# Window attention: the band mask moved to TensorE, and subtraction, copies, layer norm and mask rows moved to GpSimd

## The chip, the cores and the metric

The kernel runs on one core of one Trainium2 chip. The metric is device time in microseconds (us). One execution was profiled, and all durations of the trace come from it. TensorE (PE) has two clock levels, 1.2 and 2.4 GHz; a granted clock of 0.50 in a stretch is the lower one, 1.00 the upper.

## What is computed

Two stages follow each other, each on 8 batches of 1024 rows of width 256. The first is window attention with 16 heads of width 16, then a residual and a layer norm:

```python
scores = jnp.einsum('bhqd,bhkd->bhqk', q, k) / math.sqrt(dh)
scores = jnp.exp(scores - jnp.max(scores, axis=-1, keepdims=True))   # maximum over all 1024 keys
mask = (d <= half - 1) & (d >= -half)                                # d = j - i, half = 32
scores = jnp.where(mask, scores, 0.0)
weights = jax.nn.softmax(scores, axis=-1)                            # softmax of the exponentials
out = jnp.einsum('bhqk,bhkd->bhqd', weights, v)
x = _layernorm(x + out.transpose(0, 2, 1, 3).reshape(B, S, H * dh) @ Wo)
```

Outside the band the inner exponential is set to 0, so its own exponential is 1. The output is therefore (sum of all v + the sum over the band of (e^e^s - 1) v) divided by its mass. The second stage routes each row through three small trees and attends over the results. The change does not touch it.

## The kernel before

The work of the first stage is cut into units: unit u = 2b + g is half g (8 heads) of batch b, and one unit is 64 steps, eight steps of 128 queries for each head. Each engine has its instructions written out in one order, step by step, with semaphores between the engines. Batches 2 to 6 run in a loop, the others are written out.

In every step PE makes one `p_diff` (L529) and one `p_half` (L533), both 128x512. ScalarE (ACT) takes the positive part of `p_diff` into `above` (L615). VectorE (DVE) adds the two and takes the row maximum (L724). PE runs one `p_diff` ahead.

The rest hangs on the steps by lags. "Lag n" of head h of the unit before is step 8h + n of this unit, or step 8h + n - 64 of the one after.

- Lag 9: PE computes the window scores `p_win` (L545), 16 products of 64 columns. Each block of 64 queries sees 128 keys. The rows with the negated maxima (`m_parts`) have to be in `q_stack` before head 0's.
- Lags 10 and 11: first exponential, in two halves of 512 (L641). Lags 12 and 13: second exponential, two halves (L638).
- Lags 13 and 14: DVE computes `w_win = (p_win - 1) * window` in two halves (L758), where `window` is the 0/1 band.
- Lags 15 and 16: PE multiplies `w_win` with the values (L558, `p_pv`). Lag 18: DVE adds the value sum (L777). Lag 19, odd heads: DVE takes the reciprocal (L750), GpSimd (POOL) scales the pair into `att` (L421).

Beside this a list of jobs, `JOBS`, has one job every four steps: "m" transposes the maxima, "q", "k", "d" make the next unit's projections and split them into bf16 parts, "V" and "S" the values and their sum, "T", "O", "X" transpose `att`, project it, and transpose the next x. Job j begins at step 4j + 1 on PE. ACT and DVE follow one step later, POOL at step 4j + 4, and ACT's middle part (L627, `s_mid`) comes at step 4j + 5. For "q", "k" and "d" the POOL waits at step 4j + 4 for that middle part and then makes the low part (L398). DVE copies one part (L739), and the SP queue then loads `q_stack`, `k_stack` and `d_stack` head by head (L328).

At step 4 POOL makes two of the three bf16 parts of the negated maxima (L388, L390). At the start of the next unit SP's queue waits for them and issues three row transfers into `q_stack` (L271).

The layer norm of batch b - 2 has its statistics in unit (b - 1, 1). POOL computes `rstd` (L428, L430) at the start of unit (b, 0), and DVE normalises eight tiles of 128x256 at steps 1 to 8 (L710). SP then stores x1 and loads the next x.

## Time and profile before

| | us |
|---|---|
| median of 3 runs | 2668.9 (2658.05 to 2669.55) |
| the profiled execution's own time | 2644.6 |
| its span | 2642.8 |
| first to last row maximum (16 units) | 49.4 to 1440.8 |
| last normalisation issued | 1521.0 |
| second stage's first instruction | 1528.5 |
| PE, DVE, ACT, POOL busy | 2100.6, 1811.0, 1392.7, 659.4 |

A unit takes (1440.8 - 49.4) / 16 = 87.0 us. The time that an engine is busy is a union of its instructions' durations, so two that overlap in its pipeline count once. The median of the runs is 24.3 us above the profiled execution.

### The profile page before, as it was taken

What the parts mean: (1) busy time and instruction counts of PE and PEld (TensorE: products, weight loads), DVE (VectorE), ACT (ScalarE), POOL (GpSimd) and SP (SyncE); (2) the same over time, 40 slices, a digit from 0 to 9 for tenths busy, and PEclk for the clock granted to TensorE, in tenths of its full rate; (3) what the DMA queues carried; (4) which work ended last, traced back from release to release, by engine and by line L of the source; (5) the groups of instructions that cost most, each with busy time, mean ns of one, the idle gap of its engine ahead of it and who ended that gap; (6) DMA issues with size and microseconds to landing.
All of it is one profiled execution on the core that took longest, in us unless ns stands there. A gap on an engine that the chain in (4) does not pass through costs nothing. (4 is left out here: it accounts for less than half of the span.)

```text
span 2642.8 us, 46194 instructions
## 1 busy us (share of the span) xinstructions
PE 2100.6 (79%) x13533; PEld 1602.7 (61%) x13533; DVE 1811.0 (69%) x4451; ACT 1392.7 (53%) x2671; POOL 659.4 (25%) x920
## 2 busy tenths in 40 slices
PE   4779888788788898887888668356468848999998
PEld 2345556455555555564555657346467748999997
DVE  3667788778787787787968335536558745777775
ACT  3557667757666676676756212124246533444442
POOL 3110111101111111111100035555521135556511
PEclk8878888989888888898978555667679879999999
DMA  4624643565346435543470081699977742333311
GB/s 72 94 47 67 111 56 62 88 94 70 64 73 111 54 59 94 83 63 70 68 111 18 17 259 70 212 380 341 287 253 248 231 151 84 88 98 100 97 53 39
DMA packets 230094, 306.36 MB, mean 116 GB/s; under 512 B 44445, under 2 KB 145866, under 8 KB 229450
## 3 DMA queue, kind: packets, MB, share of 16 engines
q1 hardware_dynamic: 186746, 199.14, 37.5%
q0 software_dynamic: 22784, 67.13, 7.9%
q10 hardware_dynamic: 20304, 36.97, 3.7%
q8 instruction: 120, 1.97, 0.3%
q14 instruction: 140, 1.15, 0.1%
HBM read 129.33 MB, written 92.27 MB: 84 GB/s over the span
## 5 line engine op out<-in xcount | busy, mean ns | idle before, releaser
L724 DVE CUSTOM_DVE_ANT_0 above<-p_half,above 128x512 f32<-128x512 f32 x1024 | 691.3, 684 | 305.6 <-issue 248.1
L615 ACT ACTIVATE above<-p_diff 128x512 f32<-128x512 f32 x1024 | 599.4, 600 | 269.4 <-PE p_diff L529 267.6
L529 PE MATMUL p_diff<-d_stack,q_stack 96*128 96x512 bf16 x1024 | 433.3, 426 | 127.0 <-ACT above L615 96.0
L533 PE MATMUL p_half<-k_stack,q_stack 96*128 96x512 bf16 x1024 | 431.8, 422 | 31.0 <-DVE row_max L724 27.2
L558 PEld LDWEIGHTS p_pv<-v_win,w_win 128*128 128x128 f32 x2048 | 312.0, 225 | 78.0 <-DVE w_win L758 52.6
L558 PE MATMUL p_pv<-v_win,w_win 128*128 128x34 f32 x2048 | 307.6, 302 | 14.5 <-DVE w_win L758 13.0
L529 PEld LDWEIGHTS p_diff<-d_stack,q_stack 96*128 96x128 bf16 x1024 | 127.0, 125 | 285.3 <-ACT above L615 206.4
L1170 POOL DMA_INDIRECT raw<-sorted_y,place x192 | 206.2, 1074 | 238.5 <-DMA sorted_y<-y_tile 182.9
L641 ACT ACTIVATE p_win<-p_win 128x512 f32<-128x512 f32 x256 | 150.3, 589 | 181.5 <-PE p_win L545 179.9
L421 POOL TENSOR_TENSOR att<-total,inv 128x128 f32<-128x128 f32 x128 | 48.9, 404 | 759.2 <-DVE inv L750 759.2
L1492 ACT ACTIVATE pt_hi<-p_one 128x512 fp32r<-128x512 f32 x128 | 69.6, 595 | 259.6 <-PE p_one L1352 243.9
L758 DVE SCALAR_TENSOR_TENSOR w_win<-p_win,window 128x512 f32<-128x512 f32 x256 | 175.1, 684 | 17.9 <-ACT p_win L638 17.7
L533 PEld LDWEIGHTS p_half<-k_stack,q_stack 96*128 96x128 bf16 x1024 | 107.2, 105 | 114.7 <-DVE row_max L724 96.8
L1271 PE MATMUL p_one<-ident,x_tile 128*128 128x128 f32 x564 | 97.1, 301 | 82.2 <-DMA x_tile<-sorted_x 82.1
L545 PE MATMUL p_win<-q_stack,k_stack 99*128 99x64 bf16 x2048 | 101.2, 211 | 71.1 <-DMA q_stack<-m_parts 62.6
L638 ACT ACTIVATE p_win<-p_win 128x512 f32<-128x512 f32 x256 | 153.5, 603 | 0.0
L1663 DVE TENSOR_TENSOR tile_t_lo<-p_one,tile_t_hi 128x512 fp32r<-128x512 f32 x141 | 96.6, 685 | 80.2 <-issue 41.3
L1206 PE MATMUL p_out<-val_hi,pt_hi 128*128 128x256 f32 x512 | 150.7, 294 | 0.7 <-DVE sum L1748 0.7
L545 PEld LDWEIGHTS p_win<-q_stack,k_stack 99*128 99x128 bf16 x2048 | 90.4, 111 | 97.3 <-issue 53.2
L1206 PE MATMUL p_out<-val_hi,pt_lo 128*128 128x256 f32 x512 | 145.2, 284 | 0.0
L1206 PE MATMUL p_out<-val_lo,pt_hi 128*128 128x256 f32 x512 | 145.2, 284 | 0.0
L1416 ACT ACTIVATE tile_t_hi<-p_one 128x512 fp32r<-128x512 f32 x141 | 83.5, 592 | 112.6 <-PE p_one L1271 49.9
(217 smaller groups left out, 4857.1 us busy)
## 6 DMA issues: line engine op xcount, KB each, us to landing
x_tile<-sorted_x SPq DMA_DIRECT2D x141, 256.0 KB
sorted_y<-y_tile ACTq DMA_DIRECT2D x141, 256.0 KB
q_stack<-q_parts SPq DMA_DIRECT2D x256, 96.0 KB, 3.1
k_stack<-k_parts SPq DMA_DIRECT2D x256, 96.0 KB, 3.7
x_in<-in_L_attn_x SPq DMA_DIRECT2D x16, 1024.0 KB, 5.5
x_rows<-x POOLq DMA_DIRECT2D x16, 1024.0 KB
sorted_x<-zeros SPq DMA_DIRECT2D x51, 256.0 KB
d_stack<-d_parts SPq DMA_DIRECT2D x256, 48.0 KB, 3.7
```

What stands on the lines that cost most here:

```text
L529: nc.tensor.matmul(p_diff[s % 2][:], qs, d_stack[0:SPLIT_ROWS, h, :], start=True, stop=True).then_inc(s_diff, 1)
L533: nc.tensor.matmul(p_half[s % 2][:], qs, k_stack[g][0:SPLIT_ROWS, h, HALO + S // 2:HALO + S], start=True, stop=True).then_inc(s_half, 1)
L545: ins = nc.tensor.matmul(p_win[:, cols], k_stack[o][0:ROWS, h, WIN * i:WIN * i + P], q_stack[o][0:ROWS, h, cols], start=True, stop=True)
L558: ins = nc.tensor.matmul(p_pv[:, 2 * DV * t:2 * DV * t + 2 * DV].rearrange("p (n d) -> p n d", n=2), w_win[:, h % 2, P * t:P * t + P], v_w ...
L615: nc.scalar.activation(above[:, s % 4], p_diff[s % 2][:], ACT.Relu).then_inc(s_above, 1)
L638: nc.scalar.activation(p_win[:, cols], p_win[:, cols], ACT.Exp).then_inc(s_e2, 1)
L641: nc.scalar.activation(p_win[:, cols], p_win[:, cols], ACT.Exp, scale=DH ** -0.5).then_inc(s_e1, 1)
L724: nc.vector.tensor_tensor_reduce(out=above[:, s % 4], in0=p_half[s % 2][:], in1=above[:, s % 4], scale=1.0, scalar=-3.0e38, op0=ALU.add, o ...
L758: nc.vector.scalar_tensor_tensor(w_win[:, h % 2, cols].rearrange("p (i j) -> p i j", j=WIN), p_win[:, cols].rearrange("p (i j) -> p i j", ...
L1170: pool.indirect_dma_start(raw[b % 2][:, n, t, :], None, ys[n][:, :], bass.IndirectOffsetOnAxis(ap=where, axis=0), bounds_check=OUT_ROWS - ...
L1206: ins = nc.tensor.matmul(out_, l, r, start=first and n == 0, stop=last and n == 2)
L1271: ins = nc.tensor.transpose(p_one[j % 2][:, TILE * c + P * t:TILE * c + P * t + P], xr[:, j % X_TILES, t, P * c:P * c + P], ident[:])
```

## The change

It does five things. (1) PE adds the band mask to the window scores: for each bank of `p_win` one more product, bf16 identity times `outside` (0 inside the band, -30000 outside), repeated over 8 blocks, 512 columns. After the scale of 1/4 the first exponential gives 0 there and the second gives 1. (2) The exponentials are two instructions of 1024 columns each at lags 10 and 11, and the second writes `w_win`. POOL subtracts 1 in place, 128x1024, at lag 12, and DVE's L758 is gone. (3) The three rows of maxima go out from POOL's queue right after their parts are made. SP no longer waits for them. (4) The copies L739 move from DVE to POOL, behind L398. (5) The eight normalisations move from DVE (steps 1 to 8, one instruction each) to POOL (steps 4 to 11, a subtraction, a wait for it, and a multiplication each, both with a broadcast operand).

```diff
-EXP_LAGS = 10, 11, 12, 13
-WEIGHT_LAGS = 13, 14
+EXP_LAGS = 10, 11
+WEIGHT_LAG = 12
 @@ sync
-                    wait_alone(sp, s_mparts, u)
-                    for part in range(3):
-                        row = SPLIT_ROWS + part
-                        sp.dma_start(q_stack[1 - g][row:row + 1, :, :],
-                                     m_parts[:, part, :]).then_inc(s_mrow, 16)
 @@ gpsimd, job "m", behind m_parts
+                            pool.wait_ge(s_mparts, u)
+                            wait(pool, s_win, GH * (u - 2))
+                            alone(pool)
+                            for part in range(3):
+                                row = SPLIT_ROWS + part
+                                pool.dma_start(q_stack[1 - g][row:row + 1, :, :],
+                                               m_parts[:, part, :]).then_inc(s_mrow, 16)
 @@ gpsimd, jobs "q", "k", "d", and behind the jobs
+                            copy, of = (0, 1) if kind == "q" else (3, 2)
+                            nc.gpsimd.tensor_copy(parts[:, copy, cols], parts[:, of, cols]).then_inc(s_twice, 1)
+                    for w, o, h in late(b, g, s, WEIGHT_LAG):
+                        weights(GH * w + h, h)
                     for w, o, h in late(b, g, s, PAIR_LAG):
                         if h % 2:
                             pair(b, g, w, h // 2)
+                    if g == 0 and has(b, 2, B + 1) and 4 <= s < 4 + QT:
+                        normalise(b - 2, s - 4)
+            def normalise(b, q):
+                if q == 0:
+                    wait_alone(pool, s_rstd, b + 1)
+                row_mean = mean_var[:, q, 0:1].to_broadcast([P, C])
+                nc.gpsimd.tensor_tensor(y[:, q], y[:, q], row_mean, ALU.subtract).then_inc(s_centre, 1)
+                wait_alone(pool, s_centre, QT * b + q + 1)
+                nc.gpsimd.tensor_tensor(y[:, q], y[:, q], rstd[:, q:q + 1].to_broadcast([P, C]),
+                                        ALU.mult).then_inc(s_norm, 1)
+            def weights(k, h):
+                wait_alone(pool, s_e2, k + 1)
+                nc.gpsimd.tensor_scalar(w_win[:, h % 2], w_win[:, h % 2], -1.0, None, ALU.add).then_inc(s_ww, 1)
             batches(pool, unit)
             spread(B - 1)
+            for q in range(QT):
+                normalise(B - 1, q)
 @@ tensor, window_scores and weighted_values
-                wait(pe, s_ww, 2 * k)
+                wait(pe, s_e2, k)
+                    if i % 8 == 0:
+                        bank = p_win[:, 64 * i:64 * i + 512].rearrange("p (i j) -> p i j", j=WIN)
+                        nc.tensor.matmul(bank, ident_b[:], outside[:].unsqueeze(1).to_broadcast([P, 8, WIN]),
+                                         start=True, stop=False, skip_group_check=True)
-                pe.wait_ge(s_ww, 2 * k + part + 1)
+                if part == 0:
+                    pe.wait_ge(s_ww, k + 1)
 @@ scalar, exponential
-                    nc.scalar.activation(p_win[:, cols], p_win[:, cols], ACT.Exp).then_inc(s_e2, 1)
+                    wait(act, s_pv, k - 1)
+                    nc.scalar.activation(w_win[:, h % 2], p_win[:], ACT.Exp).then_inc(s_e2, 1)
 @@ vector
-                        normalise(b - 2, s - 1)
-                            nc.vector.tensor_copy(parts[:, copy, cols], parts[:, of, cols]).then_inc(s_twice, 1)
-                nc.vector.scalar_tensor_tensor(
-                    w_win[:, h % 2, cols].rearrange("p (i j) -> p i j", j=WIN),
-                    p_win[:, cols].rearrange("p (i j) -> p i j", j=WIN), 1.0,
-                    window[:].unsqueeze(1).to_broadcast([P, NBLK // 2, WIN]),
-                    ALU.subtract, ALU.mult).then_inc(s_ww, 1)
```

Three places show how the rows move. The first is POOL's order from step 4 to the projection jobs of unit (7, 0), which is written out; the loop has the same. Before:

```order
L388 CAST m_parts<-m_rest 64x128
L390 TENSOR_TENSOR m_parts<-m_rest,m_parts 64x128
L421 TENSOR_TENSOR att<-total,inv 128x8x16 x2
L398 TENSOR_TENSOR q_parts<-rest,q_parts 128x512
L421 TENSOR_TENSOR att<-total,inv 128x8x16 x2
```

The same place after the change, where `x_in` is the tile that is normalised (eight pairs of L447 and L449 in all, of which the first and the last stand here):

```order
L386 CAST m_parts<-m_rest 64x128
L388 TENSOR_TENSOR m_parts<-m_rest,m_parts 64x128
L395 DMA q_stack<-m_parts 1x64x128 x3
L454 TENSOR_SCALAR w_win<-w_win 128x1024
L447 TENSOR_TENSOR x_in<-x_in,mean_var 128x256
L449 TENSOR_TENSOR x_in<-x_in,rstd 128x256
...
L432 TENSOR_TENSOR att<-total,inv 128x8x16 x2
L447 TENSOR_TENSOR x_in<-x_in,mean_var 128x256
L449 TENSOR_TENSOR x_in<-x_in,rstd 128x256
L454 TENSOR_SCALAR w_win<-w_win 128x1024 x2
```

Between the maxima's parts and the first pair of `att` shown (the last head pair of an earlier unit) there are now three DMA issues, one subtraction of 1 and seven normalisations. It is the pair that job T waits for.

The second place is POOL in the stretch of the projection jobs of the same unit, after the change (before, it had the L398 rows and the pairs alone):

```order
L403 TENSOR_TENSOR q_parts<-rest,q_parts 128x512
L406 COPY q_parts<-q_parts 128x512
L454 TENSOR_SCALAR w_win<-w_win 128x1024
L403 TENSOR_TENSOR k_parts<-rest,k_parts 128x512
L406 COPY k_parts<-k_parts 128x512
L403 TENSOR_TENSOR k_parts<-rest,k_parts 128x512
L406 COPY k_parts<-k_parts 128x512
L454 TENSOR_SCALAR w_win<-w_win 128x1024
```

At steps 28 and 36 of a unit the subtraction L454 stands behind a low part and a copy, both of which wait for ACT's step 29 or 37.

The third place is PE at the window scores of one head, before and after (L529 and L556 are the same line, as are L533 and L560):

```order
L533 MATMUL p_half<-k_stack,q_stack 128x512
L545 MATMUL p_win<-q_stack,k_stack 128x64 x16
L529 MATMUL p_diff<-d_stack,q_stack 128x512
L533 MATMUL p_half<-k_stack,q_stack 128x512
L529 MATMUL p_diff<-d_stack,q_stack 128x512
```

```order
L560 MATMUL p_half<-k_stack,q_stack 128x512
L574 MATMUL p_win<-outside,ident_b 128x512
L576 MATMUL p_win<-q_stack,k_stack 128x64 x8
L574 MATMUL p_win<-outside,ident_b 128x512
L576 MATMUL p_win<-q_stack,k_stack 128x64 x8
```

Each head has two more products of 512 columns, one ahead of each eight blocks, and nothing else moves on PE.

## Rows read from the trace of the kernel before

**Rows 1.** The maximum's instruction L724 by source line.

```profile
L724 DVE CUSTOM_DVE_ANT_0 above<-p_half,above x1024: 625/691/694, 49.4 to 1440.8; 128x512 f32<-128x512 f32 x171
```

**Rows 2.** Stretches of 4 us in batch 2: busy by engine, then granted clock.

```profile
core 0: us, PE busy (x) PEld busy (x) DVE busy (x) ACT busy (x) POOL busy (x), PEclk, DMA share, GB/s
...
434.00:438.00 4.00, 2.63 (x11) 0.81 (x9) 3.88 (x11) 3.95 (x9) 0.12 (x1) 0.99 0.00 0
442.00:446.00 4.00, 4.00 (x18) 3.54 (x16) 1.75 (x6) 1.71 (x3) 1.15 (x1) 0.50 0.02 4
```

**Rows 3.** L724 alone, two records for each step, in stretches of 4 us.

```profile
431.00:435.00 4.00, 2.33 (x8) 1.00 0.00 0
443.00:447.00 4.00, 1.14 (x4) 0.50 0.00 0
```

**Rows 4.** Groups, 0 to 1350 us: busy, mean ns; idle before, its releasers.

```profile
L529 PE MATMUL p_diff<-d_stack,q_stack 96*128 96x512 bf16 x953 | 400.7, 423 | 123.4 <-ACT above L615 92.7 <-DMA d_stack<-d_parts 13.4 <-issue 12.2
L758 DVE SCALAR_TENSOR_TENSOR w_win<-p_win,window 128x512 f32<-128x512 f32 x220 | 150.3, 683 | 0.0
L641 ACT ACTIVATE p_win<-p_win 128x512 f32<-128x512 f32 x220 | 129.8, 590 | 137.5 <-PE p_win L545 136.2
L739 DVE COPY k_parts<-k_parts 128x512 bf16<-128x512 bf16 x32 | 25.4, 794 | 0.8 <-ACT k_parts L627 0.7
```

**Rows 5.** Timeline around the maxima's rows in unit (2, 1): start, us, engine.

```profile
480.03 0.42 POOL L390 TENSOR_TENSOR m_parts<-m_rest,m_parts 64x128 bf16<-64x128 f32 x1
481.53 1.08 PE L558 MATMUL p_pv<-v_win,w_win 128*128 128x34 f32 x8
488.70 1.82 SPq L271 DMA_DIRECT2D q_stack<-m_parts x3
492.36 1.03 PE L545 MATMUL p_win<-q_stack,k_stack 99*128 99x64 bf16 x16 [7.86 <-DMA q_stack<-m_parts]
```

**Rows 6.** The rows' transfers by tile: who waited, and time to landing.

```profile
  PE p_win L545: 62.6, 8
...
DMA to landing us min/median/max: 2.2/2.5/3.4
```

**Rows 7.** Timeline of unit (2, 0), steps 3 to 13.

```profile
396.82 0.28 DVE L669 SCALAR_TENSOR_TENSOR m_rest<-p_job,m_parts 64x128 f32<-64x128 f32 x1
408.46 0.20 PEld L465 LDWEIGHTS p_job<-ident,att 128*128 128x128 f32 x2 [0.64 <-POOL att L421]
```

**Rows 8.** POOL groups of the whole span.

```profile
L421 POOL TENSOR_TENSOR att<-total,inv 128x128 f32<-128x128 f32 x128 | 48.9, 404 | 759.2 <-DVE inv L750 759.2
L398 POOL TENSOR_TENSOR k_parts<-rest,k_parts 128x512 bf16<-128x512 f32 x32 | 37.3, 1166 | 122.9 <-ACT k_parts L627 122.9
L1151 POOL DMA_DIRECT2D x_rows<-x x16 | 15.1, 942 | 70.8 <-DMA sorted_x<-x_rows,slot 70.8
L408 POOL COPY v_sum<-v_sum 128x136 f32<-128x136 f32 x8 | 2.4, 296 | 0.0
L1127 POOL MEMSET w<- 128x1024 f32 x1 | 0.9, 945 | 0.0
```

**Rows 9.** Timeline of steps 29 to 31 of unit (2, 0).

```profile
426.88 0.63 ACT L627 ACTIVATE q_parts<-rest 128x512 bf16<-128x512 f32 x1
427.92 1.09 ACT L615 ACTIVATE above<-p_diff 128x512 f32<-128x512 f32 x2
429.56 1.08 PE L558 MATMUL p_pv<-v_win,w_win 128*128 128x34 f32 x8 [0.38 <-DVE w_win L758]
```

**Rows 10.** Timeline, 512-column products behind each other at granted clock 1.00.

```profile
404.72 0.38 PE L529 MATMUL p_diff<-d_stack,q_stack 96*128 96x512 bf16 x1
404.94 0.38 PE L533 MATMUL p_half<-k_stack,q_stack 96*128 96x512 bf16 x1
```

**Rows 11.** ACT's 1024-column group of the second stage.

```profile
L1387 ACT ACTIVATE w<-w 128x1024 fp32r<-128x1024 f32 x18 | 19.0, 1056 | 7.1 <-DMA b<-in_L_ffn_q_b 6.8
```

**Rows 12.** Timeline of the first stage's end.

```profile
1521.03 2.67 DVE L710 TENSOR_SCALAR x_in<-x_in,mean_var,rstd 128x256 f32<-128x256 f32 x8 [2.19 <-POOL rstd L430]
```

More of the change, by code:

```diff
@@ L113, in window_attention @@
         ones = sb("ones", [P, 1])
-        window = sb("window", [P, WIN])
+        ident_b = sb("ident_b", [P, P], BF16)
+        outside = sb("outside", [P, WIN], BF16)
         neg_half = sb("neg_half", [P, QT])
@@ L199, in window_attention @@
         s_rstd = sem("rstd_ready")
+        s_centre = sem("x1_less_mean")
         s_norm = sem("x1_ready")
@@ L264, in unit @@
                 if g == 1 and has(b, -1, 0):
[L265 to L272 removed]
+                    wait_alone(sp, s_const, 18)
                 if g == 0 and has(b, -1, 0):
@@ L347, in _ @@
             const(nc.gpsimd.memset(ident[:], 0.0))
-            const(nc.gpsimd.memset(window[:], 1.0))
+            const(nc.gpsimd.memset(outside[:], 0.0))
             pool.wait_ge(s_const, 2)
@@ L726, in unit @@
                             op0=ALU.add, op1=ALU.max, accum_out=row_max[g][:, s:s + 1]).then_inc(s_max, 1)
-                    if g == 0 and has(b, 2, B + 1) and 1 <= s <= QT:
-                        normalise(b - 2, s - 1)
                     for j, kind, i in jobs(b, g, s, 2):
@@ L731, in unit @@
                             job(b, g, j, kind, i)
-                    for j, kind, i in jobs(b, g, s, 4):
-                        if kind in PROJ:
-                            dve.wait_ge(s_mid, before(PROJ, b, g, j) + 1)
-                            parts = {"q": q_parts, "k": k_parts, "d": d_parts}[kind]
-                            copy, of = (0, 1) if kind == "q" else (3, 2)
-                            cols = slice(512 * i, 512 * i + 512)
-                            nc.vector.tensor_copy(parts[:, copy, cols], parts[:, of, cols]).then_inc(s_twice, 1)
-                    for n in (0, 1):
-                        for w, o, hh in late(b, g, s, WEIGHT_LAGS[n]):
-                            weights(GH * w + hh, hh, n)
                     for w, o, hh in late(b, g, s, TOTAL_LAG):
@@ L783, in _ @@
             batches(dve, unit)
-            for q in range(QT):
-                normalise(B - 1, q)
 NETS = 3
```

36 lines of the change are left out of this document (15 added, 21 removed).

## The prediction

> **What bounds the kernel now.** I read the instruction L724 first, because every step has one. The 16 units run from its first record to its last, 87.0 us for a unit and 1.36 us for a step [rows 1]. All that the change touches lies there, but for the first stage's last layer norm. Then I cut a batch into stretches of 4 us. The reader is to see that the bound changes within a unit, and twice over. At 434 to 438 us DVE is busy 3.88 and ACT 3.95 of 4.00 while PE has 2.63, and at 442 to 446 PE has 4.00 at granted clock 0.50 while the other two have less than half [rows 2]. Of the 45 stretches between 390 and 570 us, 20 have DVE at 3.84 or more, of which this one is an example, and PE is busy 3.38 on average in them. The maxima show what the low clock costs: 4 steps in 4 us at the high one, 2 at the low one [rows 3].
>
> Third, the groups. PE idles 92.7 us for ACT before `p_diff`, ACT idles 136.2 us for PE before the first exponential, and DVE never idles before L758 [rows 4]. So PE and ACT take turns in waiting for each other, and DVE adds its delay in its full stretches. Fourth, the waits on the maxima's rows. In unit (2, 1) the parts are ready at 480.45 us, but SP is still busy with stack loads and issues the rows at 488.70, and PE stands 7.86 us [rows 5]. Eight such waits sum to 62.6 us [rows 6]. POOL has nothing late except what it waits for.
>
> **The sum, edit by edit,** against the profiled execution.
>
> *Mask on PE.* 2 products for each of 128 heads are 256 of 512 columns. Two such behind each other start 0.22 us apart at the high clock [rows 10]; at half the clock it is twice as much. I take 0.24 on average, 62 us in all. Nothing covers it: ACT waits for these scores (the 136.2 us of rows 4). Bounds: 40 us if a third falls in PE's idle time, 75 if much is run at the low clock.
>
> *Rows from POOL.* Behind the parts POOL issues three transfers. The nearest row is POOL's own issue, 0.94 us each [rows 8], so 2.9 with a gap. The rows then land some 2.5 us later [rows 6], if POOL's queue is as quick as SP's. In unit (2, 1) they would leave until 483.4 and land at about 486. But head 7's subtraction of 1 is queued behind the issues, and PE needs it for `p_pv`, which started at 481.53 [rows 5]. It ends at 480.45 + 0.1 + 2.9 + 0.1 + 1.1 = 484.65, so this product is 3.1 late. The window scores then follow at 492.36 - 7.86 + 3.1 = 487.6, behind the landing. Eight waits: 62.6 - 8 x 3.1 = 38, and some 0.4 each for a shorter run at the low clock: -41. If POOL's transfers needed 5 us to land, 1 us of each comes back.
>
> *The 1.1 us of the subtraction* is from both sides: a memset of the same 128x1024 takes 0.945, a copy of 136 columns 0.296, and a two-input operation 1.17 for 512 columns, thus 2.3 for 1024 [rows 8]. It has one input, so I go near the memset and keep 0.95 and 2.3. The Trainium skill (GPSIMD Engine Reference, Engine selection) says that one-input elementwise work is roughly at line rate on GpSimd and two-input work about half as fast as on VectorE, which the memset and L398 bear out as far as they reach. The same page (Elementwise, side-by-side cycle accounting) gives 1.8 cycles per element for a tight loop, which at 1024 columns would be an estimated 1.5 us; the sum would then be about 25 us higher.
>
> *Normalisation on POOL.* 128 columns took 0.42 us (rows 5, L390) and 512 took 1.17 [rows 8], so 256 cost 0.67, and a tile costs 2 x 0.67 and two handoffs of 0.08: 1.5 us, against 2.67 for eight on DVE [rows 12]. In unit (b, 0) POOL now has in one row behind `m_rest`: parts 1.0, issues 3.0, subtraction 1.2, seven tiles 10.5, the last pair of `att` 0.8 [rows 8]. From 397.10 that is 413.6. Job T took that pair at 408.46, then hardly waiting (0.64) [rows 7]. So T is 5.1 late; the chain begins 0.7 earlier, since DVE has no normalisations ahead of `m_rest`; PE's clock falls in the idle time, +1.1. That is 5.5 for each of six units with scores (b = 2 to 7), 33, and 1.5 for each first half without normalisations, 3: +36. Bounds: 20 if a broadcast operand is cheap, 55 if it is not.
>
> *Copies and low parts.* At steps 28 and 36 the subtraction stands behind L398 and the copy, and these behind ACT's L627. Before, PE's `p_pv` began 2.05 us after L627's end at 427.51 [rows 9]. Now: 0.1 + 1.17 + 0.6 (the copy, from L408) + 0.1 + 1.1 = 3.07. So 1.0 late, twice in 16 units: +33, and +70 at 2.3 us for the subtraction.
>
> *DVE's relief.* L758 goes (256 x 0.68) and 80 copies (about 0.79 [rows 4]), near 235 us of work. It counts only in DVE's full stretches, and there PE's own 3.38 of 4.00 is the limit: 15.5% of 80 us, 12.4 for a batch, 99 in all. ACT is as full in 7 of the 20, so I take 60. Beside it the clock: the low stretch around 442 follows directly on the DVE-bound one, and each such stretch loses some 4 us (half the steps in 8 us [rows 3]), 64 over 16 units. The delays on POOL stand in the same stretch, so I grant only 10. Together -70, bounds 0 and -160.
>
> *Exponentials.* One of 1024 columns takes 1.056 [rows 11], two of 512 in a row 1.09 [rows 9]. 256 pairs save 9 us of ACT, but a positive part behind one waits up to 0.5 us longer: 0, within 15 either way.
>
> *End of the stage.* Eight tiles of 1.5 instead of 2.67 [rows 12], with nothing beside them: +9.
>
> Sum: 62 - 41 + 36 + 33 - 70 + 0 + 9 = +29 us. The profiled execution would go from 2644.6 to 2673.6. The median of the runs shown is 24.3 above that execution, so I forecast 2668.9 + 29 = 2698 us.
>
> **The rivals.** *The other side: DVE was the real bound and the clock stays up.* With DVE's 15 us per unit gone, the stretch at 434 to 446 never starves PE, and the mask's products fill PE more. Then the whole 64 instead of 10 comes in: 29 - 54 = -25, 2644 us. For it speaks that 20 of 45 stretches are full on DVE and that the fall comes right there [rows 2]; against it that POOL's delays are put into the same stretch. It decides from about 3 us per unit of clock gain on. *POOL is slow.* At 2.3 us a subtraction adds 1.2 us to the 32 late products (38), to the 16 behind the row issues (19), and once more in six chains (7), and dearer normalisations add 14: +78, 2776 us. L398's rate speaks for it, the memset against it. *The rows' wait stays.* If SP was not the cause but the landing, 62.6 would remain and the sum be +70, 2739. The timeline speaks against it: issue at 488.70, end of the wait 3.66 later [rows 5]. *POOL's transfers land late.* The Trainium skill (DMA: Bandwidth & Descriptors, Specifications) gives a first-byte time of about 1 us for GpSimd's queue and 0.6 for SP's; 0.4 us later changes nothing here, as the landing has 1.6 us in hand.
>
> **How the numbers follow.** The forecast case (late POOL, partial relief) 0.50, the faster rival 0.30, slow POOL 0.14, the staying wait 0.06. The range goes from below the faster rival, with ACT's 15, to the slow POOL: 2625 to 2780. What a measurement of this kernel can tell from no change is about 0.5%, 13 us. The forecast case by itself reaches from 2660 to 2740, so a part of it is no change. Faster by over 0.5%: 0.30. Within: 0.14. Slower: 0.56.
>
> **What would show it.** The window scores should have no wait on `q_stack<-m_parts`. PE should wait for POOL's `w_win` before `p_pv` once in each unit at step 7 (3 us) and twice in the projection stretch (1 us), and for `att` near 5 us in the first halves from batch 2 on. POOL's subtraction should be near 1.1 us and the normalising operations near 0.67. DVE should lose near 235 us of busy time. The time from L724's first to its last record should grow by some 20 us, and the stage's end by 9. The prediction is wrong if the granted clock no longer falls at the projection jobs, if the subtraction takes 2 us, or if PE loses the 62 us of the mask in time that it idles anyway.

## The result

Both kernels were timed in alternation on one chip, four executions each.

| | before | after |
|---|---|---|
| median, us | 2666.7 | 3020.05 (3017.5 to 3025.77) |
| ratio to before | | 1.1334 [1.1302, 1.1366] |
| span of the profiled execution, us | 2642.8 | 3015.7 |
| first to last row maximum (the 16 units), us | 1391.4 | 1734.1 |
| span without these units, us | 1251.4 | 1281.6 |

The change costs 353 us. The forecast was +29, with an upper end of 2780. The direction was right (it had a chance of 0.56) and the size was wrong by twelve times. Nearly all of it, 342.7 us, lies between the first and the last row maximum, now L752 (answers to [rows 1]; columns: count, duration min/median/max in ns, first and last start in us):

```profile
L752 DVE CUSTOM_DVE_ANT_0 above<-p_half,above x1024: 656/692/695, 54.0 to 1788.1; 128x512 f32<-128x512 f32 x171
```

A unit takes 108.4 us instead of 87.0. Of the 30.2 us outside the units, 4.6 lie ahead of the first maximum and 19.7 between the last maximum and the end of the last normalisation (82.9 before, 102.6 after), where the forecast for the stage's end was +9; the rest comes behind that.

The groups of the whole span after the change (busy us, mean ns | idle before, releasers):

```profile
L648 ACT ACTIVATE above<-p_diff 128x512 f32<-128x512 f32 x1024 | 595.6, 605 | 562.2 <-PE p_diff L556 555.9
L556 PE MATMUL p_diff<-d_stack,q_stack 96*128 96x512 bf16 x1024 | 463.2, 455 | 178.9 <-ACT above L648 153.9 <-DMA d_stack<-d_parts 13.9 <-issue 9.5
L591 PE MATMUL p_pv<-v_win,w_win 128*128 128x34 f32 x2048 | 369.9, 339 | 184.6 <-POOL w_win L454 184.0
L454 POOL TENSOR_SCALAR w_win<-w_win 128x1024 f32<-128x1024 f32 x128 | 354.7, 2771 | 248.4 <-ACT w_win L671 247.7
L574 PE MATMUL p_win<-outside,ident_b 128*128 128x512 bf16 x256 | 138.2, 540 | 3.6 <-DMA q_stack<-m_parts 3.6
L449 POOL TENSOR_TENSOR x_in<-x_in,rstd 128x256 f32<-128x256 f32 x64 | 39.3, 614 | 9.2
L395 POOL DMA_DIRECT2D q_stack<-m_parts x48 | 26.8, 561 | 9.9 <-POOL m_parts L388 9.8
L406 POOL COPY q_parts<-q_parts 128x512 bf16<-128x512 bf16 x32 | 19.6, 612 | 0.0
L695 DVE TENSOR_TENSOR rest<-d_parts 128x512 f32<-128x512 f32 x16 | 18.8, 1174 | 1.4 <-POOL k_parts L403 1.4
```

The subtraction L454 takes 2.77 us, where the prediction took 1.1 and bounded it at 2.3. PE stands 184.0 us for it before `p_pv`. "The subtraction takes 2 us" was one of the prediction's own signs of being wrong. The other prices are as forecast or lower: 0.61 us for a normalising operation (forecast 0.67), 0.61 for a copy (0.6), 0.56 for a row's issue (0.94). Who waited for `w_win` (us, times), from the view of that tile:

```profile
who waited for it (us, times):
  POOL w_win L454: 247.7, 39
  PEld p_pv L591: 211.3, 89
  PE p_pv L591: 184.0, 86
```

PE came too early for 86 of 128 heads, 2.1 us each time. The prediction had counted 48 late heads (32 in the stretches of projection jobs and 16 behind the rows' issues). Half of the 86 waits lie in these places, with 121 us of the 184; the other half, with 63 us, belongs to heads for which no wait was forecast. One of those in a stretch of projection jobs, the subtraction of step 28 (start, us, engine):

```profile
611.29 1.17 POOL L403 TENSOR_TENSOR q_parts<-rest,q_parts 128x512 bf16<-128x512 f32 x1 [0.32 <-ACT q_parts L660]
612.40 0.61 POOL L406 COPY q_parts<-q_parts 128x512 bf16<-128x512 bf16 x1
612.98 2.77 POOL L454 TENSOR_SCALAR w_win<-w_win 128x1024 f32<-128x1024 f32 x1
615.80 1.78 PEld L591 LDWEIGHTS p_pv<-v_win,w_win 128*128 128x128 f32 x8 [3.12 <-POOL w_win L454]
615.81 1.92 PE L591 MATMUL p_pv<-v_win,w_win 128*128 128x34 f32 x8 [2.63 <-POOL w_win L454]
617.54 0.62 PE L556 MATMUL p_diff<-d_stack,q_stack 96*128 96x512 bf16 x1
```

This is the queue that the prediction described, with a subtraction two and a half times as long as assumed. Behind the wait `p_diff` takes 0.62 us, where 5 us earlier it took 0.39. PE was busy 1.37 of the 4 us from 612 to 616 us, at a mean granted clock of 0.94, and from 616 to 620 it is busy 4.00 at 0.50, the lower level. Over 1000 us of each kernel (columns: busy us and count of PE, PEld, DVE, ACT and POOL, then granted clock, DMA share, GB/s), first before:

```profile
200.00:1200.00 1000.00, 847.01 (x5489) 554.79 (x5486) 790.64 (x2191) 681.40 (x1300) 117.43 (x184) 0.87 0.50 77
```

After:

```profile
200.00:1200.00 1000.00, 793.58 (x4421) 515.60 (x4421) 517.27 (x1499) 526.51 (x875) 365.38 (x351) 0.78 0.37 59
```

POOL has the longest single step and is still busy only 365 of 1000 us. No engine is full; the mean clock went from 0.87 to 0.78. DVE's busy time over the whole span fell by 187.7 us (1811.0 to 1623.3), less than the 235 forecast.

One step of the prediction came as forecast, the rows of maxima (answers to [rows 6]). The wait for `att` before job T, forecast at 5 us in each first half, did not: it was 6.7 us in all.

```profile
  PE p_win L574: 3.6, 1
...
DMA to landing us min/median/max: 2.2/3.0/6.4
```

### The profile page after: what moved, and what is told of

It reads as the page before. It is cut to its first block and busy times, and to the rows that moved or that the text cites. A ratio compares the mean times of both kernels' runs of the same rounds, so it can differ in the third digit from the quotient of the medians.

```text
span 3015.7 us, 46047 instructions
## 1 busy us (share of the span) xinstructions
PE 2327.6 (77%) x13789; PEld 1743.1 (58%) x13789; DVE 1623.3 (54%) x4051; ACT 1381.0 (46%) x2415; POOL 1164.4 (39%) x1305
## 5 line engine op out<-in xcount | busy, mean ns | idle before, releaser
L752 DVE CUSTOM_DVE_ANT_0 above<-p_half,above 128x512 f32<-128x512 f32 x1024 | 694.7, 691 | 816.7 <-issue 560.5
L556 PE MATMUL p_diff<-d_stack,q_stack 96*128 96x512 bf16 x1024 | 463.2, 455 | 178.9 <-ACT above L648 153.9
L591 PEld LDWEIGHTS p_pv<-v_win,w_win 128*128 128x128 f32 x2048 | 374.6, 265 | 264.1 <-POOL w_win L454 211.3
L591 PE MATMUL p_pv<-v_win,w_win 128*128 128x34 f32 x2048 | 369.9, 339 | 184.6 <-POOL w_win L454 184.0
L560 PE MATMUL p_half<-k_stack,q_stack 96*128 96x512 bf16 x1024 | 463.3, 452 | 10.6 <-DVE row_max L752 9.6
L454 POOL TENSOR_SCALAR w_win<-w_win 128x1024 f32<-128x1024 f32 x128 | 354.7, 2771 | 248.4 <-ACT w_win L671 247.7
L556 PEld LDWEIGHTS p_diff<-d_stack,q_stack 96*128 96x128 bf16 x1024 | 136.3, 134 | 363.1 <-ACT above L648 301.5
L1172 POOL DMA_INDIRECT raw<-sorted_y,place x192 | 211.1, 1100 | 239.6 <-DMA sorted_y<-y_tile 184.0
L674 ACT ACTIVATE p_win<-p_win 128x1024 f32<-128x1024 f32 x128 | 129.0, 1008 | 251.2 <-PE p_win L576 251.1
L576 PEld LDWEIGHTS p_win<-q_stack,k_stack 99*128 99x128 bf16 x2048 | 128.8, 121 | 64.6 <-issue 50.8
L560 PEld LDWEIGHTS p_half<-k_stack,q_stack 96*128 96x128 bf16 x1024 | 112.0, 109 | 71.9 <-DVE row_max L752 58.8
L1147 POOL DMA_INDIRECT sorted_x<-x_rows,slot x128 | 127.9, 999 | 44.1 <-issue 38.7
L574 PE MATMUL p_win<-outside,ident_b 128*128 128x512 bf16 x256 | 138.2, 540 | 3.6 <-DMA q_stack<-m_parts 3.6
L576 PE MATMUL p_win<-q_stack,k_stack 99*128 99x64 bf16 x2048 | 137.9, 223 | 0.0
```

The source lines that it names most:

```text
L454: nc.gpsimd.tensor_scalar(w_win[:, h % 2], w_win[:, h % 2], -1.0, None, ALU.add).then_inc(s_ww, 1)
L556: nc.tensor.matmul(p_diff[s % 2][:], qs, d_stack[0:SPLIT_ROWS, h, :], start=True, stop=True).then_inc(s_diff, 1)
L560: nc.tensor.matmul(p_half[s % 2][:], qs, k_stack[g][0:SPLIT_ROWS, h, HALO + S // 2:HALO + S], start=True, stop=True).then_inc(s_half, 1)
L574: nc.tensor.matmul(bank, ident_b[:], outside[:].unsqueeze(1).to_broadcast([P, 8, WIN]), start=True, stop=False, skip_group_check=True)
L576: ins = nc.tensor.matmul(p_win[:, cols], k_stack[o][0:ROWS, h, WIN * i:WIN * i + P], q_stack[o][0:ROWS, h, cols], start=False, stop=i % 8 ...
L591: ins = nc.tensor.matmul(p_pv[:, 2 * DV * t:2 * DV * t + 2 * DV].rearrange("p (n d) -> p n d", n=2), w_win[:, h % 2, P * t:P * t + P], v_w ...
```

## The experiments

Ratios are against the kernel before on the same chip. The later runs were on chips on which the kernel before took 2615 and 2619 us, not 2660 to 2667; what follows the units took some 40 us less there in several kernels. So beside the ratio each run has its **units**, the time from first to last row maximum in its profile, which is where the change works (before 1391.4, after 1734.1). They are one execution each, and that of the kernel before (2644.6 us in all) was faster than each of its four timed ones (2658 and more). In the run of the price list below, where the first stage is that of the kernel before, the units took 1407.1. So a difference of units against 1391.4 can come out 15 us too high, and where it departs from the ratio, the ratio counts.

### The price of the subtraction, by itself

The kernel before with a list of GpSimd operations ahead of its constants, each alone:

```diff
+            for _ in range(3):
+                trial(nc.gpsimd.tensor_scalar(a32[:], a32[:], -1.0, None, ALU.add))
...
+                trial(nc.gpsimd.tensor_copy(b32[:], a32[:]))
...
+                trial(nc.gpsimd.tensor_tensor(a32[:], a32[:], b32[:], ALU.add))
...
+                trial(nc.gpsimd.tensor_tensor(a32[:], a32[:], m1[:, 0:1].to_broadcast([P, 1024]), ALU.add))
```

> The kernel before with a price list at its start: GpSimd runs, each waiting for the one ahead, a subtraction of 1 as a tensor-scalar addition of 128x1024 in place, the same out of place, in place on 256 columns, a copy, a two-input addition, an addition with a broadcast column as second input, and one with the scalar from a column. If the tensor-scalar form is slow by itself, it is 2.77 us here too, alone on the chip's ports, and 0.7 us at 256 columns; if the 2.77 us come from VectorE working on the same memory at the same time, it is near 1.1 us here. The two-input addition should be near 2.3 us and the copy near 1.1 us.

Timeline of POOL (x3 rows hold three instructions and two handoffs of about 0.15 us):

```profile
2.03 0.95 POOL L362 MEMSET above<- 128x1024 f32 x1
3.37 2.80 POOL L365 TENSOR_SCALAR att<-att 128x1024 f32<-128x1024 f32 x1 [0.17 <-POOL try_m L363]
12.60 2.77 POOL L367 TENSOR_SCALAR above<-att 128x1024 f32<-128x1024 f32 x1 [0.15 <-POOL att L365]
21.37 0.85 POOL L369 TENSOR_SCALAR att<-att 128x256 f32<-128x256 f32 x1 [0.15 <-POOL above L367]
24.39 3.37 POOL L371 COPY above<-att 128x1024 f32<-128x1024 f32 x3 [0.16 <-POOL att L369]
27.91 7.30 POOL L373 TENSOR_TENSOR att<-att,above 128x1024 f32<-128x1024 f32 x3 [0.15 <-POOL above L371]
35.36 5.96 POOL L375 TENSOR_TENSOR att<-att,try_m 128x1024 f32<-128x1024 f32 x3
41.50 2.85 POOL L377 TENSOR_SCALAR att<-att,try_m 128x1024 f32<-128x1024 f32 x1 [0.18 <-POOL att L375]
```

At 1024 columns a memset takes 0.95 us, a copy 1.0, a two-input operation 2.3 (half as much, 1.17, for 512 [rows 8]), one with a broadcast column 1.9, and the one-input subtraction with a constant 2.77 into another tile and 2.79 to 3.17 in place, three times each. With the constant in a column (L377) it takes 2.85, so where the constant comes from makes little difference. So 2.8 us is what this form costs by itself, not what the other engines made of it. By the Trainium skill (GPSIMD Engine Reference, Engine selection) one-input elementwise work is roughly at line rate; the copy agrees, the subtraction of a constant does not, and the measurement decides.

### The subtraction's place and length

The changed kernel with the subtraction on DVE at lag 13:

```diff
-                nc.gpsimd.tensor_scalar(w_win[:, h % 2], w_win[:, h % 2], -1.0, None, ALU.add).then_inc(s_ww, 1)
+                        nc.vector.tensor_scalar(w_win[:, hh % 2], w_win[:, hh % 2], -1.0, None,
+                                                ALU.add).then_inc(s_ww, 1)
```

> The changed kernel with one part moved: the subtraction of 1 is made by VectorE (one instruction of 1024 columns at lag 13) instead of GpSimd. Theory A, GpSimd's subtraction is the cause (2.77 us where 1.1 was assumed, and PE stands behind it before p_pv, with the clock falling after the stalls): most of the 353 us go, the time is near 2700 us and PE's wait for w_win is near zero. Theory B, the mask's products and the wider exponentials are the cause (PE and ScalarE wait for each other longer at the window scores): the time stays above 2850 us. Theory C, the normalisation's chain on GpSimd: 2900 us or more, since it stays.

Measured 2776.43 us, ratio 1.0418 [1.0362, 1.0475], units 1499.9. Two thirds of the loss go, and PE's wait for `w_win` is 13.1 us. That is theory A in the main, but 2776 is not its "near 2700", so something else costs as well. The instruction took 0.85 us on DVE in the mean.

The changed kernel with POOL's subtraction on 384 of 1024 columns (the rest of the weights keeps its 1 too much):

```diff
-                nc.gpsimd.tensor_scalar(w_win[:, h % 2], w_win[:, h % 2], -1.0, None, ALU.add).then_inc(s_ww, 1)
+                nc.gpsimd.tensor_scalar(w_win[:, h % 2, 0:384], w_win[:, h % 2, 0:384], -1.0, None, ALU.add).then_inc(s_ww, 1)
```

> The changed kernel with GpSimd's subtraction of 1 on 384 of the 1024 columns alone; the other columns keep their exponentials as they are, so a part of the computation is left out. 384 columns should take about 1.1 us by the rate of 2.77 us for 1024, the duration that the prediction assumed. If the duration of this one instruction was the only thing wrong in the prediction, the time is within 2640 to 2740 us (its sum said +29). If other terms are wrong as well, it is above 2780 us.

Measured 2817.38, ratio 1.0559 [1.0481, 1.0636], units 1527.4. This run turned out to be the test of the prediction's whole sum, since its subtraction takes what the prediction took (1.17 us against 1.1):

```profile
L591 PE MATMUL p_pv<-v_win,w_win 128*128 128x34 f32 x2048 | 331.8, 316 | 66.0 <-POOL w_win L454 65.1 <-DVE total L781 0.8
L454 POOL TENSOR_SCALAR w_win<-w_win 128x384 f32<-128x384 f32 x128 | 149.8, 1170 | 247.0 <-ACT w_win L671 246.3
```

At its own price the sum of +29 should have been +149. So the price was one error and there was at least one more. The waits came where the prediction put them: 41 of the 46 lie in the stretches of projection jobs (1.0 and 1.8 us each) and behind the rows' issues (1.3).

The changed kernel with `p_pv` two steps later:

```diff
-WIN_LAG, TOTAL_LAG, PAIR_LAG = 9, 18, 19
+WIN_LAG, TOTAL_LAG, PAIR_LAG = 9, 19, 20
-PV_LAGS = 15, 16
+PV_LAGS = 17, 18
```

> The changed kernel with the weighted values two steps later (lags 17 and 18 for 15 and 16), the totals at lag 19 and the pair at lag 20. POOL's work is the same. Theory A, the 2.77 us of the subtraction cost because PE comes for w_win before it is ready: PE's idle time before p_pv falls from 184 us to under 60 and 130 to 220 us come back, 2800 to 2890 us. Theory G, POOL's load itself (its port, its queue) or the low clock is what costs: under 50 us come back, over 2970.

Measured 2716.59, ratio 1.0396 [1.0337, 1.0454], units 1476.3, the clock of 200 to 1200 us back at 0.89. The tile's waits now:

```profile
who waited for it (us, times):
  POOL w_win L454: 471.5, 78
...
  PE p_pv L591: 1.7, 1
```

POOL does the same work in the same 2.77 us (its busy share even rises, 432 of 1000 us), and 257.8 us of the units are gone, more than theory A gave (130 to 220). So most of the loss was latency at this place in the order and not POOL's load. What of the remaining 3.96% is load, this run does not tell. PE now waits 67.6 us for `att` before job T.

### The other parts

The changed kernel with the normalisation on DVE (steps 1 to 8, as before):

```diff
-                nc.gpsimd.tensor_tensor(y[:, q], y[:, q], row_mean, ALU.subtract).then_inc(s_centre, 1)
...
+                nc.vector.tensor_scalar(y[:, q], y[:, q], mean_var[:, q, 0:1], rstd[:, q:q + 1],
+                                        ALU.subtract, ALU.mult).then_inc(s_norm, 1)
```

> The changed kernel with the eight normalisations of a batch back on VectorE, the rest as changed. Theory A: the chain of GpSimd in the first halves gets shorter by 10 us, of which 5 to 8 us are on the path in 6 units, and the last stage is 9 us shorter: 40 to 60 us less, near 2970. Theory C (this chain is the cause): 200 us less or more, near 2800.

Measured 3005.78, ratio 1.1285 [1.124, 1.1329], units 1728.9: 5 us less in the units and 9 at the stage's end, 13 us by the ratio, where the forecast chain was 36 and its end 9. Neither theory holds. PE's wait for `att` was 6.7 us after the change. That PE was late in every unit anyway, so that the pair was there when job T came, is my reading of it.

The rows of maxima alone on POOL's queue, from the kernel before:

```diff
-                    wait_alone(sp, s_mparts, u)
...
+                            alone(pool)
+                            for part in range(3):
+                                row = SPLIT_ROWS + part
+                                pool.dma_start(q_stack[1 - g][row:row + 1, :, :],
+                                               m_parts[:, part, :]).then_inc(s_mrow, 16)
```

> The kernel before with the three rows of maxima issued from POOL's queue, nothing else. PE's wait on the rows falls from 62.6 us to under 10. If each of the eight waits costs what it is long and POOL has nothing behind the issues that PE needs: -45 to -60, ratio 0.978 to 0.983. If the eight window scores are then held by something else that was late beside them: under 10 us, ratio over 0.996.

Measured 2627.85, ratio 0.9858 [0.982, 0.9896], units 1363.8. The wait falls from 62.6 us to this:

```profile
  PE p_win L545: 23.0, 10
...
DMA to landing us min/median/max: 2.2/3.2/7.0
```

By the ratio this is -38 us, close to the forecast of 41, and between the two theories of this run. More of the wait stays (23.0 us) than the run's forecast of under 10; a landing takes up to 7.0 us here.

The mask's products alone, added to the kernel before:

```diff
+                    if i % 8 == 0:
+                        bank = p_win[:, 64 * i:64 * i + 512].rearrange("p (i j) -> p i j", j=WIN)
+                        nc.tensor.matmul(bank, ident_b[:], outside[:].unsqueeze(1).to_broadcast([P, 8, WIN]),
+                                         start=True, stop=False, skip_group_check=True)
...
-                                           q_stack[o][0:ROWS, h, cols], start=True, stop=True)
+                                           q_stack[o][0:ROWS, h, cols], start=False, stop=i % 8 == 7,
+                                           skip_group_check=True)
```

> The kernel before with the mask's two products of 512 columns per head added ahead of the window scores, and all else as it was: the window multiplication on DVE stays, the exponentials stay in halves (the mask is then redundant). Theory C, PE is the bound in the low-clock stretches and each product costs what it takes there: the 138 us that the mask was busy after the change come back almost whole, +100 to +140, ratio 1.04 to 1.05. Theory D, the mask costs what the prediction took, part of it in PE's idle time: +40 to +75, ratio 1.015 to 1.028. Theory E, the mask is nearly free and the wide exponentials are what is left of the loss: under +25, ratio under 1.01.

Measured 2705.77, ratio 1.0163 [1.0131, 1.0194], units 1436.9, +45.5 (+43 by the ratio). Theory D holds, and the prediction's bounds of 40 to 75 held; its 62 was too high. Busy time is no price: the 256 products are busy 138.2 us after the change, but the record of a product overlaps its neighbours' (0.38 us long and 0.22 apart in [rows 10]).

The 1024-wide exponentials alone, in the kernel before:

```diff
-EXP_LAGS = 10, 11, 12, 13
+EXP_LAGS = 10, 11
...
-                    nc.scalar.activation(p_win[:, cols], p_win[:, cols], ACT.Exp).then_inc(s_e2, 1)
+                    nc.scalar.activation(p_win[:], p_win[:], ACT.Exp).then_inc(s_e2, 1)
```

> The kernel before with exponentials of 1024 columns at lags 10 and 11 in the place of four halves, DVE's window multiplication still in halves at lags 13 and 14, no mask on PE. Theory C and D: 0 within 15 us, ratio 0.995 to 1.006, as the prediction had it. Theory E, a positive part queued behind a 1.05 us exponential holds PE's p_diff by 0.5 us, twice for each of 128 heads: +50 to +130, ratio 1.02 to 1.05.

Measured 2705.86, ratio 1.0153 [1.0123, 1.0183], units 1445.7, +54.3, but +41 by the ratio. So the cost is clear, and it lies between the two theories. Groups from 0 to 1350 us (answers to [rows 4], where PE idled 92.7 us for ACT):

```profile
L615 ACT ACTIVATE above<-p_diff 128x512 f32<-128x512 f32 x920 | 532.9, 600 | 322.9 <-PE p_diff L529 315.5 <-DVE row_max L723 2.0
L529 PE MATMUL p_diff<-d_stack,q_stack 96*128 96x512 bf16 x920 | 404.7, 443 | 161.1 <-ACT above L615 134.0 <-DMA d_stack<-d_parts 13.4 <-issue 12.4
```

PE idles 41 us more for the positive part, which now can stand behind an exponential twice as long, and the clock of 200 to 1200 us falls to 0.83. PE's wait for the maxima's rows fell from 62.6 to 24.5 us at the same time, so two terms of the sum touch the same time and don't simply add.

The changed kernel with subtraction, normalisation and copies on DVE, so that rows, mask and wide exponentials stay (diff as above, and `copies` back to DVE's step):

> The changed kernel with the subtraction of 1, the normalisation and the copies back on DVE: what stays of the change is the mask on PE, the 1024-wide exponentials, the rows from POOL's queue and the second exponential into w_win. The kernel with the subtraction alone on DVE took 2776. Theory C or D with dear mask: the copies and the normalisation only move 20 us between engines, 2740 to 2780, and batch period near 190 us. Theory F, what is left of the loss lies in POOL's copies and normalisations: under 2720.

Measured 2719.87, ratio 1.0213 [1.0174, 1.0252], units 1444.7. This is at the upper edge of theory F, and the interval does not part it from the theory above it. Against the kernel with the subtraction alone on DVE (1499.9), normalisation and copies on POOL cost 55.2 us of units, 55 by the ratio. Two parts of that show: PE's wait for `att` is 24.9 us there and 1.9 here, and DVE's subtraction takes 0.85 us there and 0.69 here, 20 us over 128 heads. The rest stays open.

Rows and normalisation on POOL, from the kernel before:

```diff
+                    if g == 0 and has(b, 2, B + 1) and 4 <= s < 4 + QT:
+                        normalise(b - 2, s - 4)
```

> The kernel before with the rows of maxima and the normalisations on POOL, nothing else. The kernel with the rows alone took 2628. If the prediction's chain is right, job T gets its pair of att late in eight first halves (POOL has no subtraction of 1 here): +25 to +45, 2653 to 2673. If a normalisation hides: within 10 of 2628. Taking eight normalisations off DVE may give back up to 15.

Measured 2629.01, ratio 1.0043 [1.0011, 1.0076], units 1390.1, 26.3 above the rows alone. By the ratio it is 48 us, of which some 12 lie between the last maximum and the last normalisation. The first theory holds. Job T waits for `att`, the kind of wait that was forecast (who waited for `att`):

```profile
  PE p_job L479: 29.8, 9
```

Rows and copies on POOL, from the kernel before:

```diff
-                            nc.vector.tensor_copy(parts[:, copy, cols], parts[:, of, cols]).then_inc(s_twice, 1)
+                            nc.gpsimd.tensor_copy(parts[:, copy, cols], parts[:, of, cols]).then_inc(s_twice, 1)
```

> The kernel before with the rows of maxima and the copies of one projection part on POOL, nothing else. POOL has time and nothing of PE's waits behind a copy but the stack loads: within 10 of 2628. If it costs by itself, the loads of the stacks come later and PE waits for d_stack: +15 to +45. If DVE was the bound: 2600 to 2615.

Measured 2563.29, ratio 0.9801 [0.9766, 0.9836], units 1345.7, 18.1 below the rows alone, 15 by the ratio. That is the third theory: DVE gave up 55 us of copies, which stand in the stretches of projection jobs. This is the fastest kernel of the study.

The kernel before with DVE's window multiplication on 64 of each 512 columns (the other weights are never made):

```diff
-                    w_win[:, h % 2, cols].rearrange("p (i j) -> p i j", j=WIN),
-                    p_win[:, cols].rearrange("p (i j) -> p i j", j=WIN), 1.0,
-                    window[:].unsqueeze(1).to_broadcast([P, NBLK // 2, WIN]),
+                    w_win[:, h % 2, 512 * bank:512 * bank + 64].rearrange("p (i j) -> p i j", j=WIN),
+                    p_win[:, 512 * bank:512 * bank + 64].rearrange("p (i j) -> p i j", j=WIN), 1.0,
+                    window[:].unsqueeze(1).to_broadcast([P, 1, WIN]),
```

> The kernel before with DVE's window multiplication on 64 of each 512 columns, so seven eighths of the weights are never made; all instructions, waits and lags stay. It takes about 0.5 us from each of 256, 130 us of busy time, from DVE, and nothing from PE or ACT. If the relief of DVE was worth what the prediction took (70 us for 235 us of work): -40 us, ratio near 0.985. If DVE's full stretches bound the kernel: -80 to -130, 0.95 to 0.97. If DVE's busy time is not what its stretches wait for: within 15 us, 0.995 to 1.005.

Measured 2596.01, ratio 0.99 [0.9833, 0.9966], units 1380.8. Each took 217 ns instead of 683 (rows 4, L758), so 119 us of work went, and 26 us came back by the ratio, 10.6 in the units. The interval holds a part of the first theory and of the third.

### Other places for the weighted values

Four kernels looked for a version that beats both. First, rows on POOL and `p_pv` one step later:

```diff
-PV_LAGS = 15, 16
+PV_LAGS = 16, 17
```

> The kernel with the rows alone on POOL (2628), and the weighted values one step later, at lags 16 and 17. PE idled 51 us for DVE's w_win there. If that wait is what it costs: 2585 to 2610. If the second exponential and the window multiplication are then only late beside another wait, or the products at lag 17 fall in the same step as the next head's window scores and hold p_diff: 2620 to 2645.

Measured 2656.99, ratio 1.0166 [1.012, 1.0212], units 1411.7. Slower by 48 us of units and 81 by the ratio than the rows alone, although the 51.1 us that PE's weight loads had waited for `w_win` fell to 0.2. I took the meeting of `p_pv` with the window scores in one step for the cause and tried lags 18 and 19 with the copies on POOL:

```diff
-WIN_LAG, TOTAL_LAG, PAIR_LAG = 9, 18, 19
+WIN_LAG, TOTAL_LAG, PAIR_LAG = 9, 20, 21
-PV_LAGS = 15, 16
+PV_LAGS = 18, 19
```

> The kernel before with rows and copies on POOL (ratio 0.980) and the weighted values at lags 18 and 19, the totals at 20, the pair at 21. PE idled about 25 us for w_win there. In the kernel with lags 16 and 17 that wait was gone, but the ratio rose from 0.986 to 1.017, with one of the two halves in the step of the next head's window scores. If that meeting is what cost, lags 18 and 19 do without it: 0.965 to 0.975. If any later place lengthens the way to job T or starves PE elsewhere: 0.99 to 1.02.

Measured 2677.53, ratio 1.0215 [1.0149, 1.0282], units 1464.5. This theory falls: they no longer meet, and it is 119 us of units (108 by the ratio) above the kernel with lags 15 and 16. Group from 0 to 1350 us:

```profile
L535 PE MATMUL p_half<-k_stack,q_stack 96*128 96x512 bf16 x908 | 413.9, 456 | 97.0 <-DVE row_max L726 95.8
```

PE waited 23.5 us for DVE there at lags 15 and 16, so the wait moved from `w_win` to the maxima, and job T waited 27.8 us. These two do not add up to 119; what else is in it stays open.

The same later place helps where POOL makes the weights. With late `p_pv` (lags 17 and 18) and the normalisation on DVE (the edits of these two kernels above):

> The changed kernel with the late weighted values (ratio 1.0396) and the normalisation back on DVE. PE idled 46.6 us there for POOL's att before job T. If that chain is what the normalisation costs: -35 to -60, ratio 1.017 to 1.027. If another wait takes its place: over 1.032.

Measured 2680.2, ratio 1.0261 [1.0178, 1.0344], units 1447.3, 29.0 below late `p_pv` alone (35 by the ratio), the first theory. PE's wait for `att` fell from 67.6 to 22.4 us. Then with the exponentials in halves:

```diff
-EXP_LAGS = 10, 11
-WEIGHT_LAG = 12
-PV_LAGS = 17, 18
+EXP_LAGS = 10, 11, 12, 13
+WEIGHT_LAG = 14
+PV_LAGS = 18, 19
...
+                    nc.scalar.activation(w_win[:, h % 2, cols], p_win[:, cols], ACT.Exp).then_inc(s_e2, 1)
```

> The kernel late_norm with the exponentials in halves of 512 at lags 10 to 13, the subtraction of 1 at lag 14 and the weighted values at lags 18 and 19 (totals 20, pair 21). The wide exponentials alone had cost 42 us on the kernel before. If that holds here: 0.013 to 0.018 below late_norm, so about 1.005. If POOL's later end makes new waits at job T: above late_norm.

Measured 2585.87, ratio 0.9866 [0.9803, 0.9929], units 1358.0, 89.3 below the one before it and 103 by the ratio, over twice what was expected. The edit also moves the subtraction and `p_pv`, so not all of it need be the exponentials'. Its groups from 0 to 1350 us:

```profile
L543 PE MATMUL p_diff<-d_stack,q_stack 96*128 96x512 bf16 x972 | 403.7, 418 | 76.9 <-ACT above L635 41.2 <-issue 18.1 <-DMA d_stack<-d_parts 14.0
L443 POOL TENSOR_SCALAR w_win<-w_win 128x1024 f32<-128x1024 f32 x112 | 310.6, 2773 | 148.7 <-ACT w_win L660 148.1
```

It keeps mask, slow subtraction, rows and copies of the change, and is faster than the kernel before. PE now waits 41.2 us for ACT, where late_norm had 71.0.

## Why the prediction was wrong

The profiled units, step by step from before to after. The last column is the prediction's term and how far it held. Terms that were run alone start from before; the others follow on each other. "By the ratio" is the difference of the ratios times 2663 us; one that starts from before is good to some 10 us, the others, which rest on several ratios, to 20 or 25.

| step | units, us | change | by the ratio | predicted |
|---|---|---|---|---|
| rows from POOL | 1363.8 | -27.6 | -38 | -41, right |
| mask on PE | 1436.9 | +45.5 | +43 | +62, in its bounds |
| exponentials | 1445.7 | +54.3 | +41 | 0 within 15, wrong |
| the three together, and DVE's window multiplication (175 us) replaced by its subtraction (88 us) | 1444.7 | -18.9 against their sum | +10 against their sum | a part of the relief of -70, not seen |
| normalisation and copies to POOL | 1499.9 | +55.2 | +55 | see below |
| subtraction to POOL at 1.17 us | 1527.4 | +27.5 | +37 | +33 with the low parts, less the rest of the relief |
| subtraction 1.17 to 2.77 us | 1734.1 | +206.7 | +206 | bound: +78 at 2.3 us |

The sum of the units' column is 342.7.

**"The 1.1 us of the subtraction"** is the step that failed most: the price was taken at 1.1 us, between 0.95 and 2.3, and it measured 2.77. I took the memset as the nearest row because both have one input, and the row that speaks of arithmetic, L398 at 1.17 us for 512 columns [rows 8], as a far bound. Both bounds were too low. The estimate of 1.5 us from the Trainium skill (GPSIMD Engine Reference, Elementwise, side-by-side cycle accounting) was too low as well: 2.77 in the trace.

**The count of late heads** made it worse. The prediction priced 48 heads. With 1.17 us PE waited 46 times, 1.4 us each, so at its own price the count was right. But it used the same count for the bound at 2.3 us. At 2.77 us PE waited 86 times, 184.0 us in all against 65.1. These 119 us are 58% of the 206.7: about 65 of them are longer waits in the places that the prediction named (56 to 121 us), and about 54 come from other heads (9 to 63). The rest of the 206.7 was not isolated; the clock goes from 0.85 in that kernel to 0.78 and back to 0.89 with late `p_pv`, and the reading that PE's idle time pulls it down is argued from that, not shown by itself. In this kernel the first 1.17 us of latency cost some 30 us and the next 1.6 us cost 207. A bound must be priced with its own count.

**"DVE's relief"**, -70, was not there in that size. Full stretches of DVE in the profile were taken as its bound. The kernel with seven eighths of the window multiplication left out took 119 us of work from DVE and got 10 to 26 us. Of 235 us of relief, that would be 21 to 51. The copies alone, 55 us of work in the stretches of projection jobs, gave 15 to 18, a better rate. So relief exists, and its rate is not the same everywhere; in the changed kernel it can't be told from zero, as the fourth row is +10 by the ratio. Its -18.9 in the units hangs on the fast profile of the kernel before; with 1407.1 for that it would be +12.5. The working misread its rows too: in the 20 stretches PE is busy 3.48 and not 3.38 on average, and ACT is at 3.84 or more in 4 and not in 7. With 3.48 the 99 us would be 83.

**"Exponentials: 0"** weighed 9 us saved against up to 0.5 us for a positive part and called it even. 256 such waits are up to 128 us, and 41 (by the ratio) to 54 us came. The prediction had rows for it: PE waits for ACT before `p_diff` 92.7 us already [rows 4], so an ACT instruction twice as long in that queue had no cover.

**"Normalisation on POOL"**, +36 with bounds 20 to 55, gave +26.3 in the units alone, with the wait at job T that was named. In the changed kernel it was worth 5. **"Copies and low parts"**, +33, came at 1.17 us in the places that were named, but that the whole row is of the same size is partly luck: it is net of the 108 us of subtraction that DVE gave up. The copies as such gain 18.1 us when moved alone. **"End of the stage"**, +9, was the 9 us between the change and its kernel with the normalisation on DVE, but the end grew by 19.7; the other 11 had no term.

At its own price of the subtraction the sum lacked 120 us (149 measured, 29 forecast). By the ratio the exponentials are 41 of it and the relief that did not come about 80.

**The rivals.** That of slow POOL had the right mechanism; its chance was 0.14 and its 2776 us assumed 2.3 us and the low count. That of a clock that stays up did not come: the clock fell. The rows' wait did not stay. The transfers from POOL land at 3.0 us instead of 2.5 in the median; after the change PE waits 3.6 us in all for them.

## What to carry to other kernels

Price an operation by a row of the same form, not by one with as many inputs; where there is none, put the price and the slack it must fit into side by side, and price the bound with its own count of late consumers. An instruction that is cheaper in sum but twice as long costs on a queue for which another engine already waits. Before giving up a slow engine, move its consumer: the 2.77 us subtraction cost 206.7 us at one lag, and with its consumer two steps later the kernel was as fast as with a 0.85 us subtraction on DVE at the old lags (ratios 1.0396 and 1.0418, units 23.6 us apart). It has to be tried, though: where DVE made the weights, a later `p_pv` cost 48 us of units (81 by the ratio) at one step and 119 (108) at three.

## What the runs showed of the hardware

- GpSimd's subtraction of a constant (128x1024, f32) takes 2.77 us, and 2.85 with the constant in a column, more than a two-input operation (2.3) or one with a broadcast column (1.9), and a copy takes 1.0. Three eighths of the columns take 1.17, a quarter 0.85.
- GpSimd's subtraction holds DVE back at its beginning only. DVE's two-input operation on SBUF (L695, 0.69 us alone) ran beside it 14 times after the change, beginning 0.14 to 0.66 us after it, took 0.91 to 1.45 us, and each time ended 1.57 to 1.59 us after the subtraction's beginning. With late `p_pv` it began 1.23 to 1.81 us after it, still inside its 2.77 us, and took 0.69 each time. With the subtraction on 384 columns the held ones ended 1.04 to 1.06 us after its beginning. By these ends DVE is held for about 0.9 us of 2.77, and 0.36 of 1.17 (an estimate, the ends less 0.69).

```profile
521.78 2.77 POOL L454 TENSOR_SCALAR w_win<-w_win 128x1024 f32<-128x1024 f32 x1
521.92 1.45 DVE L695 TENSOR_TENSOR rest<-d_parts 128x512 f32<-128x512 f32 x1
```

- DVE's subtraction took 0.69 us with nothing beside it, and 1.37 to 1.39, twice as long, the 28 times that POOL's low part and copy ran beside it (units 1499.9). That makes its mean of 0.85 us.
- A row transfer issued by POOL costs 0.56 us of its queue after the change. Over the runs POOL's landed in 2.2 to 7.8 us and SP's in 2.2 to 3.9.
- TensorE's mean granted clock from 200 to 1200 us was 0.78 after the change and 0.89 in the same program with `p_pv` two steps later.
